# A message-passing kernel of four graph layers: the gate sum cut into 14 groups for a pair of tiles in place of 16

## The reference

```
h = relu(layernorm(x)); x = x + segment_sum(w_edge * (sigmoid(h @ Wg + b) * (h @ W))[dst], src)   # layer 0
h = relu(layernorm(x)); x = x + segment_sum(h[src], dst) @ W1.T + b1                              # layer 1
h = relu(layernorm(x)); x = x + linear(h, segment_sum(linear(h[src], h[dst]), dst))               # layer 2
h = relu(layernorm(x)); x = x + relu(batchnorm(hypergraph_conv(h, src, dst)))                     # layer 3
```

## Time and profile before

| engine | busy us | share of the span | instructions |
|---|---|---|---|
| PE (matmul) | 2290.8 | 93% | 28669 |
| PEld (weight load) | 2020.2 | 82% | 28669 |
| DVE | 1455.0 | 59% | 3419 |
| ACT | 1278.3 | 52% | 2874 |
| POOL | 46.8 | 2% | 57 |

### The profile page before, as it was taken

How to read it: one execution, slowest core, us unless ns; L and a number is a source line. 1 busy time by engine, 2 the same in 40 slices (tenths; PEclk the granted TensorE clock), 3 DMA queues, 4 the chain that set the end, 5 groups by cost and what they waited for, 6 DMA issues and landing times.

```text
span 2472.4 us, 72177 instructions
## 1 busy us (share of the span) xinstructions
PE 2290.8 (93%) x28669; PEld 2020.2 (82%) x28669; DVE 1455.0 (59%) x3419; ACT 1278.3 (52%) x2874; POOL 46.8 (2%) x57
## 2 busy tenths in 40 slices
PE   3489999999899999999879999899998999999997
PEld 2258999988899898998768888788887888888886
DVE  8589999999899998998662333344333112122223
ACT  3399999999899998999532212222221000011112
POOL 3400000000000000000000000000000000000000
PEclk9599999999999999999989999999999999999999
DMA  7679999999999999999989999999998999999997
GB/s 199 161 167 211 211 204 205 203 216 203 200 185 213 205 205 183 211 207 206 207 207 291 291 290 290 255 259 258 257 261 210 291 291 290 266 252 250 268 271 190
DMA packets 1524466, 571.04 MB, mean 231 GB/s; under 512 B 869926, under 2 KB 1520938, under 8 KB 1524055
## 3 DMA queue, kind: packets, MB, share of 16 engines
q1 hardware_dynamic: 1520357, 561.54, 103.2%
q0 software_dynamic: 1600, 4.92, 0.7%
q10 hardware_dynamic: 2226, 0.62, 0.2%
HBM read 258.67 MB, written 92.61 MB: 142 GB/s over the span
## 4 chain that ended last, share of the span: by engine, by line
PE 62%; SPq 15%; ACT 10%; issue 5%; DMA 4%; DVE 3%; POOL 2%; DVEq 0%; ACTq 0%; POOLq 0%
PE ps L796 36%; SPq L543 7%; SPq L490 5%; ACT stage L1333 5%; ACT stage L1314 4%; PE ps L724 3%; PE ps L725 3%; PE ps L726 3%; PE ps L693 3%; DMA wt<-stage 3%; PE ps L695 3%; PE ps L694 3%; PE ps L701 2%; SPq L487 2%; PE ps L717 1%
## 5 line engine op out<-in xcount | busy, mean ns | idle before, releaser
L1333 ACT CAST stage<-ps 128x784 f16<-128x784 f32 x784 | 656.2, 837 | 18.6 <-PE ps L726 11.0
L796 PE MATMUL ps<-Ha,a_tiles 128*128 128x258 f16 x4606 | 523.7, 273 | 7.2 <-DVE Ha L1113 7.2
L724 PE MATMUL ps<-hot_c,hot_r 128*128 128x98 f16 x3136 | 501.5, 210 | 12.0 <-DVE hot_c L1035 10.0
L796 PEld LDWEIGHTS ps<-Ha,a_tiles 128*128 128x128 f16 x4606 | 449.9, 98 | 73.4 <-DVE Ha L1113 7.6
L725 PE MATMUL ps<-hot_c,hot_r 128*128 128x98 f16 x3136 | 499.4, 210 | 0.0
L726 PE MATMUL ps<-hot_c,hot_r 128*128 128x98 f16 x3136 | 497.8, 209 | 0.0
L693 PE MATMUL ps<-g_in,wt 128*128 128x128 f16 x2401 | 424.1, 220 | 24.6 <-DMA wt<-stage 16.7
L695 PE MATMUL ps<-g_in,wt 128*128 128x128 f16 x2401 | 424.2, 220 | 0.0
L694 PE MATMUL ps<-g_in,wt 128*128 128x128 f16 x2401 | 424.1, 220 | 0.0
L1314 ACT CAST stage<-ps 128x392 f16<-128x392 f32 x784 | 403.8, 515 | 35.6 <-PE ps L701 33.9
L1035 DVE TENSOR_TENSOR hot_c<-hot_c,meta 128x1568 f16<-128x1568 f16 x392 | 379.7, 969 | 0.0
(11 more groups left out here) (199 smaller groups left out, 2337.8 us busy)
## 6 DMA issues: line engine op xcount, KB each, us to landing
a_tiles<-counts_by_source SPq DMA_DIRECT2D x147, 1600.0 KB, 12.6
counts_by_source<-stage SPq DMA_DIRECT2D x49, 1600.0 KB, 8.5
meta<-edge_groups SPq DMA_DIRECT2D x26, 128.0 KB, 2.5
wt<-stage SPq DMA_TRANSPOSE x198, 6.2
gated_parts<-G SPq DMA_DIRECT2D x7, 448.0 KB, 3.9
g_in<-gated_parts SPq DMA_DIRECT2D x98, 32.0 KB, 5.9
out_x<-X SPq DMA_DIRECT2D x12, 256.0 KB
edge_table<-tab SPq DMA_DIRECT2D x1, 2448.0 KB, 10.5
```

The lines of the kernel that those rows point to most:

```text
L724: mm(into(0), rows_, codes(0), start=v == 0, stop=True, skip_group_check=True)
L796: last = mm(ps[:, sum_bank(ph, j, c), 0:PARTS], a_slot(ph, c, i), moving[:, i], start=i == 0, stop=i == TILES - 1)
L1333: a.copy(stage[:, b, 0:2 * FULL].rearrange("p (k i) d -> p k i d", k=2)[:, :, 0:TILES, u * SET_COLS:(u + 1) * SET_COLS], of).then_inc(s("h ...
```

## The change

The 49 target tiles are cut into 14 groups of 4, 3, 4, 3, 4, 3, 4 (the first half, 25 tiles) and 3, 4, 3, 4, 3, 4, 3 (the second, 24 tiles). Odd tiles have groups 0 to 6 in steps 1 to 7 and no group in step 0; even tiles have groups 7 to 13 in steps 0 to 6 and none in step 7. So two steps that follow each other, the last of an even and the first of an odd tile, have no sum on PE, and DVE has no add for them. The wait of `loaded` moves with group 0 from step 0 to step 1. The first half has 25 target tiles and the second 24 (before 24 and 25), so the two transposes by DMA have 25 and 16 blocks (before 24 and 17). `wt` has the size that it had.

```
-SUMS = 2 * TILE_HOTS
-FIRST = TILE_HOTS
-HALF_TILES = (range(0, 3 * FIRST), range(3 * FIRST, TILES))
+FIRST = TILE_HOTS - 1
+SUMS = 2 * FIRST
+SUM_STARTS = tuple((7 * g + 1) // 2 for g in range(SUMS)) + (TILES,)
+HALF_TILES = (range(0, SUM_STARTS[FIRST]), range(SUM_STARTS[FIRST], TILES))
...
 def sum_at(c, h):
-    return h if c % 2 else FIRST + h
+    return h - 1 if c % 2 else FIRST + h
+
+def has_sum(c, h):
+    return h > 0 if c % 2 else h < TILE_HOTS - 1
 
 def summed(g):
-    return range(3 * g, 3 * g + 3 if g < SUMS - 1 else TILES)
+    return range(SUM_STARTS[g], SUM_STARTS[g + 1])
...
-        wt, o = at("wt", [P, 6, WEIGHTS, len(HALF_TILES[1]), P], F16, o)
+        wt, o = at("wt", [P, 6, WEIGHTS, len(HALF_TILES[0]), P], F16, o)
...
-                        if not isinstance(n, int) or n >= 0:
+                        if has_sum(c, h) and (not isinstance(n, int) or n >= 0):
                             g = sum_at(c, h)
...
-                        if not isinstance(n, int) or n >= 0:
-                            add_some(n, sum_at(c if h >= 2 else c - 1, (h - 2) % TILE_HOTS))
+                        at_ = c if h >= 2 else c - 1, (h - 2) % TILE_HOTS
+                        if has_sum(*at_) and (not isinstance(n, int) or n >= 0):
+                            add_some(n, sum_at(*at_))
...
-                    for g in range(SUMS - 2, SUMS):
-                        add_some(GROUPS - 3, g)
+                    add_some(GROUPS - 3, SUMS - 1)
```

## The result

The changed kernel takes 2512.05 us (median of 4 runs, 2508.42 to 2514.79) against 2493.45 us for the kernel before, timed beside it (4 runs, 2490.14 to 2494.85). The ratio is 1.0079, 95% interval 1.0063 to 1.0095, so +18.6 us with 15.7 to 23.7 as its bounds: slower, and close to the predicted 2511.7 us. Its profiled execution took 2513.34 us, span 2511.5 us.

A forecast was written before the change was run, and what follows sets the result against it. PE was taken to set the pace, ACT close behind. Terms 35.2 - 3.5 + 1.3 - 14 - 1 + 0.1 were summed as +18.1 us, on 2493.6 giving 2511.7 us; 8-in-10 range 2494 to 2532.

The forecast's parts named there:

- The bound: Building stage: PE sets the pace, ACT is close behind, and the DMA chain is late once per pair of tiles.
- The gap: Two successive steps without a sum, even to odd tile: 1.73 us each, +35.2 us over 22 with two at loop returns.
- the other steps' stalls: PE's stalls for ACT outside the steps without a sum: 0.06 and 0.11 us less a tile, together -3.5 us.
- the walk: Hand-worked PE and ACT timeline from unit 14 through unit 3 to the end of the first sum, giving 1.73 us.
- The loop's returns: Tiles 24 to 25 and 36 to 37: PE stands 5.2 us there anyway, so the emptied steps cost 0.3 us each.
- The wait for the transposes: PE's wait ahead of group 0 moves one step later and vanishes: -14 us, bounds -9.7 and -15.
- -1 in tile 3: Tile 3, ahead of the profiled window, loses a transpose wait and gets some 0.5 us of ACT's pace: -1 us.
- Does the wait come back elsewhere?: ACT's low part of unit 0 awaits the same transposes: hidden by 0.8 us, so no cost.
- Sums, DVE, after the loop: Four more target tiles summed before the last transfers +1.3 us; DVE's two fewer adds nothing; last pair after the loop +0.1.
- the third: Rival: granted clock falls in the steps without a sum, 1 us x 22, 2534 us; chance 0.06.
- The first: Rival: transpose waits are larger in timed runs, so the change removes 33 us, not 14: 2493 us; chance 0.12.
- the gap is free: Rival: ACT, rested by groups of four, lets PE through the two steps without a sum: -17 us, 2476 us; chance 0.11.

The follow-up runs named there:

- the groups of four and two: Kernel before with its 16 groups cut mostly 4, 2, 4, 2 in place of 3 each, same sums and adds: 2524.22 us, ratio 1.0128.
- the lighter ACT: Changed kernel with ACT's high parts of units 14, 15, 0, 1, 2 around each gap cut to 24 of 49 target tiles: 2493.46 us.
- by halves: Separate semaphores for each half's transposes, PE waiting for the second half only at its first group: kernel before 2473.78 us, changed kernel 2504.73 us.
- second profile of before: Kernel before, unchanged, profiled once more: 2489.94 us, span 2488.1 us.
- the comparison without late transposes: Changed kernel against kernel before, both with separate semaphores for each half's transposes: +31.0 us.
- the store last: Store of the counts issued after all four transposes of a tile instead of between them: kernel before 2508.27 us, changed kernel 2527.32 us.
- the idle matmuls: Changed kernel with 18 matmuls of unread result added in each of the two steps without a sum: 2527.29 us, ratio 1.0138.
- the second profile of after: Changed kernel, unchanged, profiled once more: 2511.94 us, span 2510.1 us.

## Why the prediction was right, and what in it was not

**The bound.** Right. PE sets the pace with ACT close behind, shown by the groups of four and two (+32 us with the same work) and by the lighter ACT (-19 us).

**The gap, less the other steps' stalls.** Predicted 1.73 - 0.06 - 0.11 = 1.56 us a pair, measured 1.64 to 1.65 with the waits out of the way. For 20 gaps that is 31 us against 33. In parts: the walk of the gap holds to 0.05 us a step, and by halves, where no transpose is late, PE stands 1.72 us a gap for the 1.73 of the walk (mean of the 20). The saving in the other steps isn't there. (Its terms, 23 x 0.06 + 22 x 0.11, add up to 3.8 us, not to the 3.5 that the prediction wrote; by its own terms the sum was +17.8.) Over the 20 pairs away from the loop's returns the units outside the gap stand 13.6 us in odd tiles and 13.8 in even ones in the second profile of before, 13.6 and 13.9 in the first of after (14.3 and 14.4 in its second). They only moved, as walked: 0.15 us in step 3 and 0.43 in step 5 of each tile, walked 0.19 and 0.52. So an avoided stall does let the lag stand, as the prediction said, but by all of it.

**The loop's returns.** Predicted +0.3 us each. In the comparison without late transposes the pairs 24 and 25, 36 and 37 came out 1.2 and 1.0 us shorter, in the changed kernel itself 1.1 and 2.6 us longer (means of two profiles each). So +0.3 each was wrong in the changed kernel, and the stand of 2.46 us in tile 37 is most of the difference. It isn't a wait for a transfer; the other runs place it. Counted from the weight load behind the loop's own stand, it comes 54 loads later in both profiles of the changed kernel, in its version with the store last (1.39 us) and in the one by halves (0.31 us); 53 loads later with groups of four and two; 24 loads later with the idle matmuls. In these last two the load that stands belongs to a unit's twelve matmuls, which read no transposes, and with the idle matmuls it stands in the middle of a unit, where the program waits for nothing (weight loads in order of time, the first with groups of four and two, the second with the idle matmuls):

```profile
983.65 0.10 PEld L727 LDWEIGHTS ps<-hot_c,hot_r 128*128 128x128 f16 x1 [2.25 <-issue]
...
986.71 0.10 PEld L731 LDWEIGHTS ps<-hot_c,hot_r 128*128 128x128 f16 x1 [2.83 <-issue]
```

So it is a second stand that goes with the loop's return. The kernel before as it was, with the store last and by halves doesn't have it, nor has the changed one with the lighter ACT; why is open. What follows it differs as well: tile 37 is 1.6 us shorter in the second profile of after, where the granted clock is 1.00 over the 4 us behind the stand of 2.41 us, and 0.57 behind that of 2.46 us in the first.

**The wait for the transposes.** This is the term that was most mis-sized: -14 us and -1 in tile 3. By the traces the stage got 25.5 us longer (means of both profiles of each), and 30.1 us where the waits are out of play, so they gave back 4.6 us. By the medians it is 18.6 - 31.0 = -12.4 us, but those are from two chips, on which the kernel before differed by 3.4 us. Either way it is less than 15. In tile 3 nothing came back: its wait of 1.0 us went and a gap of 1.0 us took its place. In the -14 us two things were wrong.

First, of the stands ahead of the first sum not all was waiting for transposes. In the looped odd tiles of the changed kernel, 13, 25 and 37 aside, the first sum starts 0.23 to 0.29 us (0.34 once) after the last of the twelve instead of the 0.05 of other groups, with no transfer late; in the written-out tiles, where the same eight waits compare with constants, it is 0.05; with six waits in the loop (by halves) it is 0.14. So some 0.2 us in the 16 looped tiles with such a stand, 3 to 4 us of the 13.6, was no wait for a transfer, and it only moved by a step; with the store last, too, 16 stands of 3.6 us in all were left in the kernel before. That it is PE's sequencer working through the waits of `loaded` is the likely reading, from the three counts, and isn't shown by itself.

Second, a stand is worth less than its length. By halves nearly all of the stands ahead of the first sum are gone, 13.6 us (15.2, the mean of two profiles, against 1.5, each above the 0.05 of other groups), and the stage of the kernel before got 9.6 us shorter. The missing 4 us are PE's stands for ACT, which grew from 46.2 to 50.4 us: while PE stands for a transpose, ACT clears its lag. A part of them is in the even tiles 22, 30 and 46, 0.5 to 0.6 us longer than the others of their kind, where ACT's low part of unit 0 now waits for the transposes (0.67, 0.72 and 0.63 us) and PE for that.

**Does the wait come back elsewhere?** Right for the change itself, but barely: no wait of ACT for `wt<-stage` in the list of its first profile, two of 0.2 us each in the second. The tiles came out shorter than the 22.9 us from which the cover of 0.8 us was worked out (even ones 22.2). That the cover is thin was right: it was gone in the kernel with the lighter ACT (2.2 us), and gone for the store with the store last (10.8 us).

**Sums, DVE, after the loop.** Tile 48 is 1.0 us longer, as 1.3 us for four more target tiles. From the stage's end to the end of the kernel it is 1268.7 and 1267.1 us for 1266.9 and 1270.2 before: nothing. DVE's two adds fewer are nothing, as predicted: it waits 50 us more than before. The Trainium skill (VectorE: DVE Perf Modes, on the TRN2 errata) would have fewer and larger adds pay; the trace agrees with the fixed part (350 adds take 218.1 us, the 400 of before took 226.2, where the prediction's estimate was 7 us less) and shows that on an engine with time to spare it pays nothing.

**The rivals.** The clock in the gaps stayed 1.00, so the third falls; the Trainium skill's rule on micro-idle PE (TensorE: Matmul & The Clock Gate, "A second HAM failure mode") would have it swing, and here stands of 0.3 us between units in every gap didn't. The first fell with the second profile of before: of its 19.4 us, 13.3 lie outside the stage and 2.4 in it, the rest is spread between runs. The prediction had carried the 19.4 us over without a row for them; it fitted because the first profile was the odd one, for no reason that the prediction gave. That the gap is free is refuted by the 1.65 us.

**The sum.** +18.1 predicted, +18.6 (15.7 to 23.7) in the medians, +22.0 and +23.4 between the spans of the second profile of before and the two of after. The agreement to 1 us is luck beyond what the steps deserve: gap and groups were 3 us too high (33.0 for 30.1), the waits 3 to 10 us too favourable, and the spans of those profiles differ by 3 to 5 us more than the medians do, within the interval.

Of what was to be seen: waits for ACT of about 80 us (74.7), high parts at 1.08 and 1.40 us (1.08 and 1.35 to 1.47), those of units 2 and 3 not before 5.9 and 7.0 us (5.91 and 6.99), DVE's wait grown, the clock at 1.00: all so. None over 0.3 us at the first sum: not so, 2.46 us in tile 37, 0.52 in 25 and 0.39 in 13. The stage 18 us longer: 24 to 27.

## What to carry to other kernels

Where two engines hand each other buffers with two or three in flight, balance has to hold step by step. Work taken out of two steps and put into others cost here about what the other engine needs longer in the emptied steps (ACT 4.64 us, PE 3.14, so 1.5 us; 1.65 was measured), though no engine's total changed. A late transfer was better met by waiting only for the part that is needed (16 us gained here) than by emptying a step so that the work that needs it comes later (19 us lost). When a wait is put to "issue", compare it with the same code where nothing can be late before counting it as removable.

## What the runs showed of the hardware

The granted clock stayed at 1.00 with PE standing 0.3 us several times in each gap, and in the first profile of before also with its stands of up to 1.7 us. Behind the stands of 4 to 6 us at the loop's returns it fell each time, to 0.50 to 0.68 over the next microseconds. Behind single stands of 2 to 2.5 us it went either way: 0.60 over 4 us after 2.13 us in the second profile of before (which cost its tile 3 us in all), 0.57 after 2.46 us in the first profile of after, 1.00 after 2.41 us in the second and 1.00 after 2.25 us with groups of four and two.

A return of the loop can bring a second stand of PE, 53 or 54 weight loads behind the first in five profiles (0.3 to 2.5 us in tile 37) and 24 behind it in one (2.8 and 3.3 us), in two of the six at loads that read no transposes. Ahead of the first sum eight waits whose values the loop counts (in registers) go with 0.2 us of standing in the loop, six with 0.09, and the same eight against constants in written-out code with none. Adding 2 us of matmuls to each gap of a PE that waits cost 0.3 us where the clock was 1.00, and 5.7 us in the pair at one return of the loop, where the second stand came with it.
